# Mamba kernel on one core: the B and C rows rounded and split per half, straight from PSUM, with new orders for five queues

## The chip, the cores and the metric

The kernel runs on one core of one Trainium2 chip. The metric is the device time of one execution in microseconds (us). Before the change it is 4034.65 us, the median of three runs (4034.6 to 4036.17).

## What is computed

The reference normalises the input (4 batches of 1024 tokens, 128 features), runs two Mamba blocks over it, one forward and one over the reversed tokens, and then a transformer of six layers. The change touches the Mamba blocks alone. Cut to what matters, one of them is:

```python
xp, z = split(x @ W_in.T)                     # 256 channels each
xc = silu(causal_conv4(xp) + b_conv)
dt, Bm, Cm = split(xc @ W_x.T, [8, 24])       # 8 columns of dt, 16 of B, 16 of C
dt = softplus(dt @ W_dt.T + b_dt)
A = -exp(A_log)                               # 256 x 16
h = h * exp(dt_t * A) + (dt_t * u_t) * B_t    # per token, 256 channels x 16 states
y_t = sum over the 16 states of h * C_t
out = (y + xc * D) * silu(z) @ W_out.T
```

## The kernel before

Four batches in two directions are eight sequences of 1024 tokens, worked one behind the other; odd ones read the tokens backwards. Channels lie on partitions in two halves (h = 0, 1) of 128, tokens in the free dimension, as two PSUM banks (c = 0, 1) of 512. The recurrence runs per state: sequence s has states n = 0 to 15, and g = 16 s + n numbers them all. For each g:

- TensorE spreads the row of B for this state to all 128 partitions, into a pair of banks (`b_rows`, L345, the matmul in `row`, L341). The row lies in the tile `bc` as float32r, rounded, on partitions 0 to 31, and the rest that the rounding cut off on partitions 32 to 63; the matmul with `pick_r` adds the two.
- VectorE multiplies the pair with `dtx` for each half (`drive_half`, L488, stages dr0 and dr1). The product of half 1 goes back into the pair; that of half 0 goes to the tile `drive` in SBUF, or, for the states listed in `DRIVE_IN_PSUM`, into the other pair of banks.
- ScalarE makes the decays exp(dt * A) (`decays`, L455, stages dec0 and dec1), up to four states ahead.
- VectorE scans over the tokens (`scan`, L499, stages sc0 and sc1).
- SP fetches the row of C from HBM, spread over the partitions (`spread_c`, L284, stage cd); GpSimd multiplies the scanned state with it (`read_out`, L534, stages rd0 and rd1); TensorE adds the product to the output `y_ps` with the identity as weights (`add_read`, L362, stages y0 and y1).

Once per sequence come the projections on TensorE: x with its four taps (stages x00 to x11, half and bank), z, the B, C and dt columns (`project_bc`, L323, stages bc0 and bc1), dt (dt00 to dt11), the skip term (sk0, sk1), the output (o0, o1). ScalarE copies these out of PSUM (ax, az, abc), makes silu and softplus (abs, relu, ex, ln). GpSimd adds and multiplies for dt and dtx (ar0, tx0, ar1, tx1). VectorE gates y (gm0, gm1) and adds the output to the residual (ao0, ao1). SP stores the C rows to HBM (cst).

The B and C columns take this way: `take_bc` (L422) copies both banks from PSUM into the SBUF tile `x_dbl`; `round_bc` (L428) casts 64 partitions of 1024 columns of it into `bc`; `split_bc` (L482) subtracts, on partitions 32 to 63, the rounded values from those of `x_dbl`, with both inputs in SBUF. Then `b_rows` of the sequence may run.

Each engine's order is written out by hand as a list for one sequence (`MAMBA_PE`, `MAMBA_ACT`, `MAMBA_DVE`, `MAMBA_POOL`, `MAMBA_SP`, L104 to L147). An entry is (lag, state, stage): in round i it stands for sequence i - lag; `mamba_sequence` unrolls it. The engines work strictly in this order, and `after` puts the semaphore waits in front of each stage. A stage's two halves share one semaphore, counted in the order of the list. `mamba_slots` deals out four PSUM banks in TensorE's order: `b` alternates between the two pairs, a single projection takes a bank of the pair that the last `b` did not take, and whoever takes a bank waits for its last reader. For a projection that reader is named in `single`; for `bc0` and `bc1` it is `abc0` and `abc1`.

```python
for name, k in pe:
    other = 1 - pair
    if name == "b":
        pair = k % 2
        take("b", k, [2 * pair, 2 * pair + 1], ("sc1", k))
        if k % D_STATE in DRIVE_IN_PSUM:
            take("dr0", k, [2 - 2 * pair, 3 - 2 * pair], ("sc0", k))
    elif name in single:
        take(name, k, [2 * other + turn[other]], (single[name], k))
```

`read` and `state` have two buffers per half: rd of g waits for y of g - 2, sc of g for rd of g - 2. `mamba` is called once, at L1483; the transformer follows behind one more layer norm.

Of the kernel before, what the change touches and what calls it, by code (L numbers as in the profile page):

```python
# [43 lines left out]
def layer_norm_block(nc, ctx, sems, number, ones_mean, eps_col, src, out, work, finish, place=None, store=None):  # L44
# [70 lines left out]
MAMBA_ACT = [  # L115
# [74 lines left out]
def mamba(nc, xn, resid, c_rows, weights):  # L190
    win, wtap, wx, wdt, wout, packed, ident, pick = weights
    with ExitStack() as ctx:
# [64 lines left out]
        def banked(name, f):  # L257
            return {f"{name}{c}": f(c) for c in range(HALF_BANKS)}

        def halved(name, f):  # L260
            return {f"{name}{h}": f(h) for h in range(HALVES)}
# [1332 lines left out]
```

## Time and profile before

| | us |
|---|---|
| median of three runs | 4034.65 |
| the profiled execution | 4035.77 |
| its span, first to last instruction | 4034.0 |
| busy in the span: TensorE, VectorE, ScalarE, GpSimd | 3731, 3368, 2919, 3210 |
| Mamba: first drive of VectorE to the end of its last scan | 119.6 to 1085.3 |

The layer norms ahead of Mamba and the start of its first sequence fill the first 120 us; the transformer takes the rest, from about 1124 us on. The mean granted clock of TensorE over the span is 0.966 of full speed. In the rows below, a line of the timeline gives the start, the duration from the first start to the last end, the engine, the source line, the tiles written and read, the number of instructions merged in it, and in brackets the idle time before it and what ended it. Matmuls of 32 bits appear as two records each, so one bank of one projection with a full set of weights is two records, and `y` of one state and half is four.

### The profile page before, as it was taken

What the parts mean: (1) busy time and instruction counts of PE and PEld (TensorE: products, weight loads), DVE (VectorE), ACT (ScalarE), POOL (GpSimd) and SP (SyncE); (2) the same over time, 40 slices, a digit from 0 to 9 for tenths busy, and PEclk for the clock granted to TensorE, in tenths of its full rate; (3) what the DMA queues carried; (4) which work ended last, traced back from release to release, by engine and by line L of the source; (5) the groups of instructions that cost most, each with busy time, mean ns of one, the idle gap of its engine ahead of it and who ended that gap; (6) DMA issues with size and microseconds to landing.
All of it is one profiled execution on the core that took longest, in us unless ns stands there. A gap on an engine that the chain in (4) does not pass through costs nothing.

```text
span 4034.0 us, 110584 instructions
## 1 busy us (share of the span) xinstructions
PE 3731.3 (92%) x43424; PEld 2523.7 (63%) x43424; DVE 3367.5 (83%) x3440; ACT 2918.9 (72%) x6887; POOL 3209.6 (80%) x2362
## 2 busy tenths in 40 slices
PE   5898888888749999999999999999999999999997
PEld 2333333333337777777777777777777777677775
DVE  3799999999858887888878888888878888788885
ACT  4554555544338887888878888788888888788885
POOL 0777787777658888888888888888888888888883
PEclk8899899998879999999999999999999999999999
DMA  1121222122100000000000000000000000000001
GB/s 43 63 74 69 68 69 74 63 75 73 68 30 16 2 16 2 6 13 2 16 2 9 10 15 2 2 16 2 15 2 6 13 3 15 2 6 2 2 2 43
DMA packets 30703, 102.12 MB, mean 25 GB/s; under 512 B 4580, under 2 KB 6504, under 8 KB 29296
## 3 DMA queue, kind: packets, MB, share of 16 engines
q1 hardware_dynamic: 30192, 95.05, 6.9%
q8 instruction: 352, 5.77, 0.6%
q14 instruction: 159, 1.30, 0.1%
HBM read 90.32 MB, written 4.72 MB: 24 GB/s over the span
## 4 chain that ended last, share of the span: by engine, by line
PE 66%; issue 2%; ACT 2%; POOL 0%; DVE 0%; POOLq 0%; ACTq 0%; DVEq 0%
PE ps L979 16%; PE ps L909 13%; PE ps L968 9%; PE ps L920 8%; PE ps L956 7%; PE ps L1004 5%; PE ps L1017 3%; PE ps L941 1%; PE ps L931 1%; PE ps L986 1%; PE ps L992 1%; ACT prob L1110 0%; PE ps L891 0%; ACT mixed L1119 0%; ACT sq L1072 0%
## 5 line engine op out<-in xcount | busy, mean ns | idle before, releaser
L1365 POOL TENSOR_TENSOR resid<-resid,sq 128x1024 f32<-128x1024 f32 x384 | 909.1, 2373 | 4.2 <-DVE sq L1219 3.7
L537 POOL TENSOR_TENSOR read<-state,c_row 128x1024 f32<-128x1024 f32 x256 | 687.4, 2703 | 202.8 <-DVE state L503 132.7
L1387 POOL TENSOR_TENSOR resid<-resid,rnorm 128x1024 f32<-128x1024 f32 x384 | 725.2, 1904 | 17.8
L979 PE MATMUL ps<-mixed,w_vo 128*128 128x128 f32 x6144 | 719.1, 275 | 3.0 <-ACT mixed L1119 2.3
L979 PEld LDWEIGHTS ps<-mixed,w_vo 128*128 128x128 f32 x6144 | 709.9, 192 | 12.9 <-issue 4.6
L909 PE MATMUL ps<-w_qk,xs_parts 128*128 128x512 f32 x2304 | 639.9, 413 | 48.9 <-issue 18.9
L1110 ACT ACTIVATE prob<-ps,stat 128x64 f32<-128x64 f32 x3072 | 655.4, 384 | 0.5 <-DVE stat L1239 0.4
L1219 DVE TENSOR_TENSOR sq<-ps,rope_l 128x1024 f32<-128x1024 f32 x384 | 462.7, 1205 | 124.6 <-ACT sq L1072 124.6
L367 PE MATMUL mamba_ps<-read,ident 128*128 128x512 f32 x1024 | 521.3, 648 | 23.3 <-POOL read L537 23.0
L1232 DVE TENSOR_TENSOR resid<-ps,rope_l 128x1024 f32<-128x1024 f32 x384 | 464.8, 1210 | 71.8 <-ACT sq L1072 64.4
L909 PEld LDWEIGHTS ps<-w_qk,xs_parts 128*128 128x128 f32 x2304 | 413.6, 191 | 165.6 <-issue 82.3
L1072 ACT ACTIVATE sq<-ps 128x1024 f32<-128x1024 f32 x384 | 396.3, 1032 | 156.4 <-PE ps L909 122.1
L1394 POOL TENSOR_TENSOR prob<-prob,stat 128x1024 f32<-128x1024 f32 x192 | 365.8, 1905 | 167.6 <-DVE stat L1250 167.6
L1119 ACT COPY mixed<-ps 128x512 f32<-128x512 f32 x768 | 400.1, 603 | 112.9 <-PE ps L968 112.8
L1196 DVE TENSOR_REDUCE ssq<-sq 128x16 f32<-128x1024 f32 x384 | 465.9, 1213 | 8.9 <-ACT sq L1072 4.3
L920 PE MATMUL ps<-ident,resid 128*128 128x128 f32 x3072 | 414.8, 275 | 14.0 <-ACT w_vo L1054 13.1
L503 DVE TENSOR_TENSOR_SCAN state<-decay,mamba_ps 128x1024 f32<-128x1024 f32 x176 | 396.5, 2276 | 4.2
L920 PEld LDWEIGHTS ps<-ident,resid 128*128 128x128 f32 x3072 | 351.6, 141 | 75.5 <-issue 60.8
L968 PE MATMUL ps<-prob_t,rows 32*128 32x512 f32 x3072 | 386.2, 613 | 4.4 <-DVE xb L1267 1.6
L367 PEld LDWEIGHTS mamba_ps<-read,ident 128*128 128x128 f32 x1024 | 196.8, 203 | 294.3 <-issue 245.5
L459 ACT ACTIVATE decay<-dt,neg_a 128x1024 f32<-128x1024 f32 x256 | 279.5, 1143 | 97.6 <-DVE state L503 97.5
L1094 ACT COPY q_t<-ps 128x512 f32<-128x512 f32 x384 | 231.4, 603 | 124.7 <-PE ps L920 122.5
(140 smaller groups left out, 5724.7 us busy)
## 6 DMA issues: line engine op xcount, KB each, us to landing
c_row<-c_rows SPq DMA_DIRECT2D x128, 512.0 KB, 3.6
w_stage<-w_qk_hbm SPq DMA_DIRECT2D x6, 1024.0 KB, 4.9
vo_stage<-w_v_hbm SPq DMA_DIRECT2D x6, 512.0 KB, 3.8
vo_stage<-w_o_hbm SPq DMA_DIRECT2D x6, 512.0 KB, 4.6
xn<-x_hbm SPq DMA_DIRECT2D x4, 512.0 KB, 5.5
kept<-resid SPq DMA_DIRECT2D x8, 256.0 KB, 2.9
resid<-kept SPq DMA_DIRECT2D x8, 256.0 KB, 4.3
out_hbm<-resid SPq DMA_DIRECT2D x8, 256.0 KB, 2.0
```

What stands on the lines that cost most here:

```text
L367: last = pe.matmul(y_ps[h][:, c, :], ident[:, :], read[:, h, g % 2, cols(c)], start=False, stop=n == LAST)
L537: pool.tensor_tensor(read[:, h, g % 2, :], state[:, h, g % 2, :], c_row[:, g % C_AHEAD, :], ALU.mult).then_inc(done[f"rd{h}"], 1)
L909: last = pe.matmul(ps[:, A + c, :], xs_parts[:, odd, xpart, :], w_qk[:, wpart, cols], start=k == 0, stop=k == 2)
L920: last = pe.transpose(bank[:, j * P:(j + 1) * P], qk[:, tile % 2, col:col + P], ident[:, :])
L968: last = pe.matmul(banks[w], rows[rows_w, tile % 2, own, :], prob_t[rows_w, tile % 2, :, own, :], start=own == 0, stop=own == 1)
L979: last = pe.matmul(bank[:, 0:P], w_vo[:, l % 2, head_at(place_h), :], mixed[:, odd, place_h, :], start=place_h == 0, stop=place_h == HEADS ...
L1110: last = act.activation(prob[:, tile % 2, place_h, :], score_ps[:, place_h, :], ACT.Exp, bias=stat[:, tile % 2, 0, place_h:place_h + 1])
L1196: dve.tensor_reduce(ssq[:, tile % 2, part * HEADS:(part + 1) * HEADS, 0], sq[:, 0, :].rearrange("p (h d) -> p h d", d=HEAD_DIM), AX_X, ALU ...
L1219: dve.tensor_tensor(sq[:, 1 + part, :].rearrange("p (h s d) -> p h s d", s=2, d=HEAD_DIM // 2), swapped, table(part, 1, tile).rearrange("p ...
L1232: dve.tensor_tensor(qk[:, tile % 2, part * INNER:(part + 1) * INNER].rearrange("p (h d) -> p h d", d=HEAD_DIM), heads_ps.rearrange("p (h d ...
L1365: pool.tensor_tensor(qk[:, tile % 2, cols], qk[:, tile % 2, cols], sq[:, 1 + part, :], ALU.add).then_inc(done[f"rotated{part}"], 1)
L1387: pool.tensor_tensor(heads, heads, norms, ALU.mult).then_inc(done[f"normed{part}"], 1)
```

## The change

`round_bc` and `split_bc` now work bank by bank and read the PSUM bank of the projection: the cast (stages abch0, abch1) takes 64 partitions of 512 columns from PSUM, and the split (stages split0, split1) subtracts in two halves, with one input in PSUM and one in SBUF. `take_bc` stays, for the dt rows and the C rows. The banks of bc0 and bc1 are held until the split has read them. All five orders are new, and the list of states whose drive goes to PSUM has five members instead of six. In the diff the orders are cut: TensorE's, GpSimd's and SP's as they are after, VectorE's before and after, ScalarE's left out.

```diff
 MAMBA_PE = [
+    (2, 8, "y0"), (1, None, "dt11"), (1, None, "dt10"), (2, 11, "b"), (2, 8, "y1"), (2, 12, "b"), (2, 9, "y0"),
+    (2, 9, "y1"), (2, 10, "y1"), (2, 10, "y0"), (2, 13, "b"), (2, 11, "y0"), (2, 12, "y0"), (2, 14, "b"), (2, 11, "y1"),
+    (0, None, "x01"), (2, 13, "y0"), (2, 15, "b"), (2, 12, "y1"), (2, 13, "y1"), (2, 14, "y0"), (1, 0, "b"),
+    (2, 14, "y1"), (0, None, "x10"), (2, 15, "y0"), (1, 1, "b"), (0, None, "x11"), (2, 15, "y1"), (1, 2, "b"),
+    (0, None, "x00"), (1, None, "sk0"), (1, 3, "b"), (1, 0, "y0"), (2, None, "o1"), (1, None, "sk1"), (1, 0, "y1"),
+    (1, 4, "b"), (1, 1, "y0"), (1, 1, "y1"), (0, None, "z01"), (2, None, "o0"), (1, 2, "y1"), (1, 5, "b"), (1, 2, "y0"),
+    (0, None, "z00"), (1, 6, "b"), (1, 3, "y1"), (0, None, "bc1"), (0, None, "bc0"), (1, 3, "y0"), (1, 4, "y0"),
+    (1, 7, "b"), (1, 4, "y1"), (0, None, "z10"), (0, None, "dt00"), (1, 5, "y1"), (1, 8, "b"), (0, None, "dt01"),
+    (1, 5, "y0"), (0, None, "z11"), (1, 6, "y0"), (1, 9, "b"), (1, 6, "y1"), (1, 7, "y1"), (1, 7, "y0"), (1, 10, "b")]
...
 MAMBA_DVE = [
-    (1, 1, "dr0"), (1, 1, "dr1"), (2, None, "gm0"), (2, None, "gm1"), (1, 1, "sc1"), (1, 1, "sc0"), (1, 2, "dr0"),
-    (1, 2, "dr1"), (2, None, "ao1"), (1, 2, "sc1"), (1, 2, "sc0"), (1, 3, "dr0"), (1, 3, "dr1"), (2, None, "ao0"),
-    (1, 3, "sc1"), (1, 3, "sc0"), (1, 4, "dr0"), (1, 4, "dr1"), (1, 4, "sc0"), (1, 4, "sc1"), (1, 5, "dr0"),
-    (1, 5, "dr1"), (1, 5, "sc1"), (1, 5, "sc0"), (1, 6, "dr0"), (1, 6, "dr1"), (1, 6, "sc1"), (1, 6, "sc0"),
-    (1, 7, "dr0"), (1, 7, "dr1"), (1, 7, "sc1"), (1, 7, "sc0"), (1, 8, "dr0"), (1, 8, "dr1"), (1, 8, "sc1"),
-    (1, 8, "sc0"), (1, 9, "dr0"), (1, 9, "dr1"), (1, 9, "sc0"), (1, 9, "sc1"), (1, 10, "dr0"), (1, 10, "dr1"),
-    (1, 10, "sc0"), (1, 10, "sc1"), (1, 11, "dr0"), (1, 11, "dr1"), (1, 11, "sc0"), (1, 11, "sc1"), (1, 12, "dr0"),
-    (1, 12, "dr1"), (1, 12, "sc1"), (1, 12, "sc0"), (1, 13, "dr0"), (1, 13, "dr1"), (0, None, "split"), (1, 13, "sc1"),
-    (1, 13, "sc0"), (1, 14, "dr0"), (1, 14, "dr1"), (1, 14, "sc0"), (1, 14, "sc1"), (1, 15, "dr0"), (1, 15, "dr1"),
-    (1, 15, "sc0"), (1, 15, "sc1"), (0, 0, "dr0"), (0, 0, "dr1"), (0, 0, "sc0"), (0, 0, "sc1")]
+    (1, 3, "sc0"), (1, 4, "dr0"), (1, 3, "sc1"), (1, 4, "dr1"), (1, 4, "sc1"), (2, None, "ao0"), (1, 4, "sc0"),
+    (1, 5, "dr0"), (1, 5, "dr1"), (1, 5, "sc1"), (1, 5, "sc0"), (1, 6, "dr0"), (1, 6, "dr1"), (0, None, "split1"),
+    (1, 6, "sc0"), (0, None, "split0"), (1, 6, "sc1"), (1, 7, "dr0"), (1, 7, "dr1"), (1, 7, "sc1"), (1, 7, "sc0"),
+    (1, 8, "dr0"), (1, 8, "dr1"), (1, 8, "sc1"), (1, 8, "sc0"), (1, 9, "dr0"), (1, 9, "dr1"), (1, 9, "sc0"),
+    (1, 9, "sc1"), (1, 10, "dr0"), (1, 10, "sc0"), (1, 10, "dr1"), (1, 10, "sc1"), (1, 11, "dr0"), (1, 11, "dr1"),
+    (1, 11, "sc0"), (1, 11, "sc1"), (1, 12, "dr0"), (1, 12, "dr1"), (1, 12, "sc0"), (1, 12, "sc1"), (1, 13, "dr0"),
+    (1, 13, "dr1"), (1, 13, "sc0"), (1, 13, "sc1"), (1, 14, "dr0"), (1, 14, "dr1"), (1, 14, "sc1"), (1, 14, "sc0"),
+    (1, 15, "dr0"), (1, 15, "dr1"), (1, 15, "sc0"), (1, 15, "sc1"), (0, 0, "dr0"), (0, 0, "dr1"), (0, 0, "sc0"),
+    (0, 0, "sc1"), (0, 1, "dr0"), (0, 1, "dr1"), (1, None, "gm0"), (0, 1, "sc1"), (0, 1, "sc0"), (0, 2, "dr0"),
+    (0, 2, "dr1"), (1, None, "gm1"), (0, 2, "sc1"), (0, 2, "sc0"), (0, 3, "dr0"), (1, None, "ao1"), (0, 3, "dr1")]
...
 MAMBA_POOL = [
+    (1, 5, "rd0"), (1, 6, "rd0"), (1, 6, "rd1"), (1, 7, "rd1"), (1, 7, "rd0"), (1, 8, "rd1"), (1, 8, "rd0"),
+    (1, 9, "rd0"), (1, 10, "rd0"), (0, None, "ar0"), (1, 9, "rd1"), (1, 10, "rd1"), (0, None, "tx0"), (1, 11, "rd0"),
+    (1, 11, "rd1"), (1, 12, "rd0"), (0, None, "ar1"), (1, 12, "rd1"), (1, 13, "rd0"), (1, 13, "rd1"), (1, 14, "rd0"),
+    (1, 14, "rd1"), (0, None, "tx1"), (1, 15, "rd0"), (0, 0, "rd0"), (1, 15, "rd1"), (0, 0, "rd1"), (0, 1, "rd1"),
+    (0, 1, "rd0"), (0, 2, "rd0"), (0, 2, "rd1"), (0, 3, "rd0"), (0, 3, "rd1"), (0, 4, "rd1"), (0, 4, "rd0"),
+    (0, 5, "rd1")]
...
 MAMBA_SP = [
+    (1, 5, "cd"), (1, 6, "cd"), (1, 7, "cd"), (1, 8, "cd"), (0, None, "cst"), (1, 9, "cd"), (1, 10, "cd"), (1, 11, "cd"),
...
-DRIVE_IN_PSUM = (4, 9, 10, 11, 14, 15,)
+DRIVE_IN_PSUM = (9, 11, 12, 13, 15,)
...
-    single = {f"bc{c}": f"abc{c}" for c in range(2)} | {f"o{c}": f"ao{c}" for c in range(2)} | {
+    single = {f"bc{c}": f"split{c}" for c in range(2)} | {f"o{c}": f"ao{c}" for c in range(2)} | {
...
-                    after(pe, ("split", g // D_STATE))
+                    after(pe, ("split0", g // D_STATE), ("split1", g // D_STATE))
...
-                        after(act, (f"bc{c}", s), ("split", s - 1), ("cst", s - 1), *[(f"dt{h}{k}", s - 1) for h in range(HALVES) for k in range(2)])
+                        after(act, (f"bc{c}", s), ("cst", s - 1), *[(f"dt{h}{k}", s - 1) for h in range(HALVES) for k in range(2)])
-                def round_bc(s):
-                    after(act, ("abc0", s), ("abc1", s), ("b", D_STATE * (s - 1) - 1))
-                    act.copy(bc[:, s % 2, :], x_dbl[0:BC_ROWS, :]).then_inc(done["abch"], 1)
+                def round_bc(c):
+                    def stage(s):
+                        after(act, (f"bc{c}", s), ("b", D_STATE * (s - 1) - 1))
+                        act.copy(bc[:, s % 2, cols(c)], bank(f"bc{c}", s)[0:BC_ROWS]).then_inc(done[f"abch{c}"], 1)
+                    return stage
...
-                          **banked("abc", take_bc), "abch": round_bc, **parts("abs", take_dt("abs", ACT.Abs, dt)),
+                          **banked("abc", take_bc), **banked("abch", round_bc), **parts("abs", take_dt("abs", ACT.Abs, dt)),
...
-                def split_bc(s):
-
-                    low = bc[32:64, s % 2, :]
-                    after(dve, ("abch", s))
-                    dve.tensor_tensor(low, x_dbl[32:64, :], low.bitcast(F32), ALU.subtract).then_inc(done["split"], 1)
+                def split_bc(c):
+
+                    def stage(s):
+                        low = bc[32:64, s % 2, cols(c)]
+                        after(dve, (f"abc{c}", s), (f"abch{c}", s))
+                        dve.tensor_tensor(low, bank(f"bc{c}", s)[32:64], low.bitcast(F32), ALU.subtract).then_inc(done[f"split{c}"], 1)
+                    return stage
...
-                stages = {"split": split_bc, **halved("dr", drive_half), **halved("sc", scan),
+                stages = {**banked("split", split_bc), **halved("dr", drive_half), **halved("sc", scan),
```

## Rows read from the trace of the kernel before

**Rows 1.** VectorE's groups from first to last scan, 119.5 to 1086 us: busy, mean ns, idle

```profile
L495 DVE TENSOR_TENSOR mamba_ps<-dtx,mamba_ps 128x1024 f32<-128x1024 f32 x176 | 215.9, 1227 | 27.5 <-PE mamba_ps L342 7.8
...
L503 DVE TENSOR_TENSOR_SCAN state<-decay,drive 128x1024 f32<-128x1024 f32 x80 | 184.3, 2304 | 1.5 <-ACT decay L459 1.5
...
L495 DVE TENSOR_TENSOR drive<-dtx,mamba_ps 128x1024 f32<-128x1024 f32 x80 | 97.0, 1213 | 20.6 <-PE mamba_ps L342 14.3
...
L486 DVE TENSOR_TENSOR bc<-x_dbl,bc 32x1024 fp32r<-32x1024 f32 x7 | 19.7, 2820 | 0.2
...
L524 DVE SCALAR_TENSOR_TENSOR resid<-mamba_ps,resid 128x512 f32<-128x512 f32 x14 | 9.6, 685 | 0.0
```

**Rows 2.** Timeline of VectorE in one sequence, from 607: start us, us, what, count

```profile
607.04 1.20 DVE L495 TENSOR_TENSOR drive<-dtx,mamba_ps 128x1024 f32<-128x1024 f32 x1
...
613.95 1.19 DVE L495 TENSOR_TENSOR drive<-dtx,mamba_ps 128x1024 f32<-128x1024 f32 x1
...
623.27 1.22 DVE L495 TENSOR_TENSOR drive<-dtx,mamba_ps 128x1024 f32<-128x1024 f32 x1
...
630.96 1.22 DVE L495 TENSOR_TENSOR drive<-dtx,mamba_ps 128x1024 f32<-128x1024 f32 x1
...
653.01 1.22 DVE L495 TENSOR_TENSOR drive<-dtx,mamba_ps 128x1024 f32<-128x1024 f32 x1
...
660.29 1.22 DVE L495 TENSOR_TENSOR drive<-dtx,mamba_ps 128x1024 f32<-128x1024 f32 x1
...
682.59 2.59 DVE L495 TENSOR_TENSOR mamba_ps<-dtx,mamba_ps 128x1024 f32<-128x1024 f32 x2
...
689.68 2.59 DVE L495 TENSOR_TENSOR mamba_ps<-dtx,mamba_ps 128x1024 f32<-128x1024 f32 x2
...
696.55 1.20 DVE L495 TENSOR_TENSOR drive<-dtx,mamba_ps 128x1024 f32<-128x1024 f32 x1
...
703.80 1.22 DVE L495 TENSOR_TENSOR drive<-dtx,mamba_ps 128x1024 f32<-128x1024 f32 x1
...
706.42 2.82 DVE L486 TENSOR_TENSOR bc<-x_dbl,bc 32x1024 fp32r<-32x1024 f32 x1
709.26 2.29 DVE L503 TENSOR_TENSOR_SCAN state<-decay,mamba_ps 128x1024 f32<-128x1024 f32 x1
...
713.65 2.57 DVE L495 TENSOR_TENSOR mamba_ps<-dtx,mamba_ps 128x1024 f32<-128x1024 f32 x2
...
727.59 1.20 DVE L495 TENSOR_TENSOR drive<-dtx,mamba_ps 128x1024 f32<-128x1024 f32 x1
```

**Rows 3.** Timeline of GpSimd and VectorE around two instructions with both inputs in SBUF

```profile
671.09 2.37 POOL L537 TENSOR_TENSOR read<-state,c_row 128x1024 f32<-128x1024 f32 x1 [1.49 <-PE mamba_ps L367]
...
672.44 3.16 DVE L503 TENSOR_TENSOR_SCAN state<-decay,drive 128x1024 f32<-128x1024 f32 x1
...
701.57 6.58 POOL L537 TENSOR_TENSOR read<-state,c_row 128x1024 f32<-128x1024 f32 x2 [1.99 <-DVE state L503]
```

**Rows 4.** Timeline of VectorE: its first drive, its first scan, its last two scans

```profile
119.59 1.22 DVE L495 TENSOR_TENSOR drive<-dtx,mamba_ps 128x1024 f32<-128x1024 f32 x1 [8.81 <-PE mamba_ps L342]
...
123.63 2.29 DVE L503 TENSOR_TENSOR_SCAN state<-decay,drive 128x1024 f32<-128x1024 f32 x1 [1.45 <-ACT decay L459]
...
1080.84 4.46 DVE L503 TENSOR_TENSOR_SCAN state<-decay,mamba_ps 128x1024 f32<-128x1024 f32 x2
```

**Rows 5.** Timeline of TensorE: records behind gaps and without, in brackets the idle before

```profile
483.50 6.65 PE L311 MATMUL mamba_ps<-xn,wtap 128*128 128x512 f32 x8 [1.40 <-DVE state L503]
...
688.14 5.42 PE L367 MATMUL mamba_ps<-read,ident 128*128 128x512 f32 x12
...
1026.70 1.19 PE L342 MATMUL mamba_ps<-bc,pick_r 64*128 64x512 f32 x2 [4.65 <-DVE state L503]
1027.82 7.58 PE L367 MATMUL mamba_ps<-read,ident 128*128 128x512 f32 x12
```

**Rows 6.** Timeline of TensorE at the start: x projections ahead of the first B rows

```profile
107.85 10.18 PE L311 MATMUL mamba_ps<-xn,wtap 128*128 128x512 f32 x16
```

More of the change, by code:

```diff
@@ L104 @@
 MAMBA_PE = [
[10 rows of a table removed]
-MAMBA_ACT = [
[10 rows of a table removed]
-MAMBA_DVE = [
[10 rows of a table removed]
-MAMBA_POOL = [
[6 rows of a table removed]
[9 rows of a table added]
+MAMBA_ACT = [
[10 rows of a table added]
+MAMBA_DVE = [
[10 rows of a table added]
+MAMBA_POOL = [
[6 rows of a table added]
 MAMBA_SP = [
-    (1, 1, "cd"), (1, 2, "cd"), (1, 3, "cd"), (1, 4, "cd"), (1, 5, "cd"), (1, 6, "cd"), (1, 7, "cd"), (1, 8, "cd"),
-    (1, 9, "cd"), (1, 10, "cd"), (1, 11, "cd"), (1, 12, "cd"), (0, None, "cst"), (1, 13, "cd"), (1, 14, "cd"),
-    (1, 15, "cd"), (0, 0, "cd")]
-DRIVE_IN_PSUM = (4, 9, 10, 11, 14, 15,)
+    (1, 5, "cd"), (1, 6, "cd"), (1, 7, "cd"), (1, 8, "cd"), (0, None, "cst"), (1, 9, "cd"), (1, 10, "cd"), (1, 11, "cd"),
+    (1, 12, "cd"), (1, 13, "cd"), (1, 14, "cd"), (1, 15, "cd"), (0, 0, "cd"), (0, 1, "cd"), (0, 2, "cd"), (0, 3, "cd"),
+    (0, 4, "cd")]
+DRIVE_IN_PSUM = (9, 11, 12, 13, 15,)
 MAMBA_EXPS = ("dec0", "dec1", "ex0", "ex1", "ln0", "ln1")
```

36 rows, old and new, of tables (MAMBA_ACT, MAMBA_PE, MAMBA_POOL) are left out of this document.

## The prediction

> **What bounds the kernel now.** The change touches the Mamba part alone, so I first looked for its place in the span and for its bound. The view of instruction groups, kept to VectorE and to the stretch from the first to the last of its scans, gives few idle microseconds [rows 1]: in about 966 us the drives waited 27.5 and 20.6 us, the split 0.2. Most of that is semaphore gaps of 0.1 us; 7.8 and 14.3 us (8.8 of them ahead of the first drive) are waits for TensorE's B rows. The 80 scans of a drive in SBUF took 184.3 us, 2.7 more than 80 times 2.27. So VectorE sets the time: 256 states' worth of drive, drive, scan, scan, one behind the other. GpSimd, ScalarE and TensorE matter only where they make it wait.
>
> The timeline of VectorE shows how regular that is [rows 2]. I write dr0(g) for the first drive of state g and take the step from one dr0 to the next. From 607.04 to 727.59 is one whole sequence, 120.55 us. The steps depend only on the order within the state and on where the drive lies:
> - SBUF, scan 0 before scan 1, next drive in SBUF: 6.91 (607.04 to 613.95).
> - SBUF, scan 1 before scan 0: 7.28 (653.01 to 660.29); with two gates 9.32 (613.95 to 623.27), with one output add 7.69 (623.27 to 630.96).
> - PSUM, followed by PSUM 7.09, followed by SBUF 6.87 (682.59, 689.68, 696.55).
> - The state with the split: 9.85 (703.80 to 713.65). Its split and gap take 2.84, of which 0.05 replace a gap that would be there anyway, so without it 7.06: that is also the step of an SBUF state followed by a PSUM one.
>
> **The change, part by part.**
>
> *The split.* Before, one instruction of 1024 columns with both inputs in SBUF: 2.79 us net per sequence, 2.82 busy [rows 1, 2]. Of these 1.7 are not work: GpSimd's pair of reads that began at 701.57 ended at 708.15, and only then did the split (begun 706.42) get on, for the last 1.1 us [rows 2, 3]. The scan at 672.44 shows the same: two SBUF inputs, 3.16 us instead of 2.29, while GpSimd was in a read until 673.46 [rows 3]. Drives, with one input in PSUM, never stretch like that. After, two instructions of 512 columns with one input in PSUM; the nearest row is the output add, PSUM and SBUF in, 512 columns: 685 ns [rows 1]. How they stand between their neighbours matters. In the row, a scan starts 0.02 us after the split's end (709.24 to 709.26), whereas an independent neighbour on all partitions overlaps by 0.09 (two scans end 4.46 after 1080.84, not 4.58 [rows 4]). With these gaps on both sides one half costs 0.83, two 1.66. Were the halves to overlap like the others, two would cost 1.22; both ends go into the range. I take 1.66, for it is what this operation showed. Gain 1.13 per sequence. The first split lies ahead of the first drive, so 7 count: **-7.9 us**.
>
> The Trainium skill (VectorE: DVE Perf Modes, section Two Vector instructions with no wait between them) speaks against the halves here: an instruction whose operands start in another group of 32 partitions than the last one's is held until all before it are done, and the split starts at partition 32. The row's gap of 0.02 instead of an overlap agrees, and by the rule each half breaks the overlap twice; without the rule the sum would be 3.1 us lower (7 times 0.44).
>
> *The steps.* Without gates, outputs and splits, before: one 6.91, six of 7.28, three each of 7.06, 7.09 and 6.87, together 113.65. After: drives of five states instead of six are in PSUM (9, 11, 12, 13, 15). States 0 and 6 have scan 0 first (13.82), 1, 2, 5, 7 are 7.28 (29.12), 8 and 14 7.06 (14.12), 11 and 12 7.09 (14.18), 9, 13 and 15 6.87 (20.61), state 10, interleaved, about 7.25, states 3 and 4, interleaved so that scan 1 of state 3 stands behind dr0 of state 4, about 14.1. Sum 113.2, 0.45 less, 8 times: **-3.6 us**. Gates and outputs: before 2.04 and twice 0.41; after, the two gates stand apart (about 0.95 each) and one output lies where it covers no gap: 2.9 against 2.86, nothing.
>
> *What the timeline waits for.* Before there were 13.3 us of waiting for B rows and 2.7 us of stretched scans, 16.0 in eight sequences [rows 1]. The new orders of five queues remove them all in their old places (**-16.0**) and make new ones. I looked for these by laying the new orders of TensorE and GpSimd beside VectorE's steps.
> - State 13. `b_rows(12)` waits for scan 0 of state 11, which ends 4.75 us behind dr0(11). Between `b_rows(11)` and it TensorE has one `y` to add, 2.5 us of work at most, so it idles 2.3 us or more. Behind it stand four `y`, 16 records, and then `b_rows(13)`. At full clock: 0.63 and 16 times 0.45 (12 records took 5.42) and 0.7, so the rows are ready 13.5 us behind dr0(11); they are due at 14.16. But after such gaps the granted clock falls to the lower of its two levels, 1.2 of 2.4 GHz: behind an idle 4.65 us the B rows and 12 records took 1.12 and 7.58 where 0.63 and 5.42 is usual [rows 5], 2.65 more. That would be a wait of 2.0. I take 1.1 per sequence, between 0 and 2.0, since the gap here is nearer half as long.
> - State 15. `b_rows(14)` waits likewise, then come `y1(11)`, the four taps of `x01` (8 records), `y0(13)`: the same 16 records, due 13.93 us behind dr0(13), ready at 13.5. At the low clock 2.2 us late. The gap ahead is only 1.3 us; one x run after 1.40 us took 6.65 for its 8 records [rows 5], others did not. I take 0.6.
> - State 0. GpSimd has `tx1` ahead of `rd0(15)` and ends this read 2.83 us behind dr0(0), where the scan of an SBUF drive wants to start at 2.47. It waits, as at 672.44: 0.35.
> Together 2.05 per sequence: **+16.4 us**.
>
> *What I cost at nothing.* The two casts straight from PSUM (512 columns each, in place of one of 1024) lie on ScalarE beside the scans. The banks of `bc0` and `bc1` are now held until the splits, and `b_rows(7)` waits for the second; a scan of 2.2 us covers its 0.7 us. Without that cover it would be 0.8 us a sequence. On SP the store of the C rows moves from behind `cd(12)` to behind `cd(8)`; `cd(9)` stands behind it, but it has a state's time, and what it waits for (`abc0`) is older by then. Waits for `split` on TensorE become two on one semaphore. The two relu and abs of the last dt part move; `b_rows(11)` now waits for them, due 7.25 us behind dr0(10), with about 1 us to spare at full clock. The tail behind the last scan (at 1085.3 [rows 4]) is in the same order.
>
> *The start.* Before the first drive TensorE ran two x projections of the second sequence, 10.18 us, and the first drive stood 8.81 us waiting for B rows [rows 4, 6]. After, one of them stands there; but all four parts of dt are read ahead of it, with ScalarE's softplus between. Between -5.1 (half of 10.18) and 0, I take **-1.3**, near 0 because the longer chain of ScalarE takes most of it. The first scan then waits for its decay as before (1.45 [rows 4]).
>
> Sum: -7.9 - 3.6 - 16.0 + 16.4 - 1.3 = -12.4. The profiled execution took 4035.77 us (span 4034.0 and 1.8 around it), 1.1 above the median of the three runs. That gives 4023.4; as the runs lie a little lower, **4023**.
>
> **The rivals.**
> 1. *TensorE keeps its pace.* The new order fills the gap ahead of the x projection of state 0 with `y1(14)` (before, TensorE stood 1.40 us there and slowed [rows 5]), and the waits at 13 and 15 don't come. Then new waits are 0.35 times 8, 2.8: -26, 4010. Against it: the gaps ahead of `b_rows(11)`, `(12)` and `(14)`.
> 2. *TensorE's slow pace decides (slower).* Every long gap is followed by the low clock: 2.0 at state 13, 2.2 at state 15, about 1 at state 11, where dt, abs and relu now stand ahead of the B rows, and 0.35: 5.5 per sequence, 44 in all, +15, 4051. It is slower from new waits of 3.6 us a sequence on (28.8 in 8). For it: slack of 0.4 to 0.7 us only, against 2.65 lost per gap.
> 3. *A read gets in ahead of scan 0 of state 6.* That scan has an SBUF drive and starts 3.07 us behind dr0(6), as `rd0(5)`, released by `y0(3)`, starts at about 3.05 to 3.2. If GpSimd is first, the scan waits 2.3 us in each sequence: +18.4 on my sum, 4042.
> 4. *The split from PSUM is not freed of GpSimd.* Then each half waits for a read like the old one, 1.7 us, 14 times 1.7: +11.8, 4047. Against it: no drive ever stretched.
>
> **How the numbers follow.** Forecast 0.43, rival 1 0.25, rival 2 0.15, rival 3 0.12, rival 4 0.05. A measurement of this kernel tells about 0.2% (8 us) from no change. Faster by more: all of rival 1 and 0.32 of the forecast, 0.57. Within: 0.11 of the forecast, 0.10 of rival 3, 0.04 of rival 2: 0.25. Slower: 0.11, 0.02 and rival 4, 0.18. The range goes from 4008, rival 1 with the overlapping halves in part, to 4044, beyond rival 3; it leaves out most of rivals 2 and 4.
>
> **What would show it.** The split should have 16 instructions near 690 ns and none longer; a mean over 1 us is rival 4. The step of state 6 should be near 8.6, that of states 1 and 2 near 8.2. VectorE's waits for B rows should fall at dr0(13) and dr0(15); if they are absent and the whole sequence takes 118 us, it is rival 1. Scans of an SBUF drive over 3 us at state 6 are rival 3. A sequence above 121 us with low granted clock ahead of states 11 to 15 is rival 2. The forecast's mechanism is wrong if the split's gain is seen but the waits lie at other states.

## The result and the profile after

The changed kernel takes **4060.85 us** (median of four runs, 4058.78 to 4071.12), 1.0070 times the kernel before in the same session, 95% interval 1.0052 to 1.0088. That is 0.7% slower; 4023 was forecast, 4044 was the upper end. The profiled execution has a span of 4057.0 us against 4034.0.

Three points of VectorE's timeline split the difference of 23.0 us: the end of the last scan, the first reciprocal of the transformer's 192 tiles, and the end.

| | before | after | difference |
|---|---|---|---|
| start to end of the last scan | 1085.30 | 1071.42 | -13.9 |
| to the first reciprocal | 109.07 | 107.29 | -1.8 |
| from there to the end | 2839.6 | 2878.3 | **+38.7** |

Mamba, the only part that the change touches, got 13.9 us faster. The transformer, whose code is the same, got slower by 38.7. First Mamba. VectorE's groups from its first drive to its last scan (117.9 to 1071.5 us), answering [rows 1]:

```profile
L506 DVE TENSOR_TENSOR_SCAN state<-decay,mamba_ps 128x1024 f32<-128x1024 f32 x168 | 379.1, 2276 | 6.6 <-ACT decay L460 1.2 <-issue 0.4
L498 DVE TENSOR_TENSOR mamba_ps<-dtx,mamba_ps 128x1024 f32<-128x1024 f32 x168 | 205.7, 1225 | 28.2 <-PE mamba_ps L341 10.9 <-DVE state L506 0.5 <-DVE mamba_ps L498 0.5
L506 DVE TENSOR_TENSOR_SCAN state<-decay,drive 128x1024 f32<-128x1024 f32 x88 | 202.1, 2297 | 2.2 <-ACT decay L460 1.3
L498 DVE TENSOR_TENSOR drive<-dtx,mamba_ps 128x1024 f32<-128x1024 f32 x88 | 106.5, 1210 | 26.4 <-PE mamba_ps L341 19.6 <-DVE state L506 0.5
...
L488 DVE TENSOR_TENSOR bc<-mamba_ps,bc 32x512 fp32r<-32x512 f32 x14 | 9.6, 684 | 0.4
```

The halves of the split take 684 ns each. The 19.6 us are the wait ahead of the first drive alone; it is counted from the end of the first splits, and these now end at 98.5 us, far ahead of it (before, at 110.8). Waits for B rows inside the sequences are the 10.9 us. VectorE's timeline of one sequence around the split, and around the one state where it waits, answering [rows 2]:

```profile
641.21 1.22 DVE L498 TENSOR_TENSOR drive<-dtx,mamba_ps 128x1024 f32<-128x1024 f32 x1
642.56 1.23 DVE L498 TENSOR_TENSOR mamba_ps<-dtx,mamba_ps 128x1024 f32<-128x1024 f32 x1
643.82 0.68 DVE L488 TENSOR_TENSOR bc<-mamba_ps,bc 32x512 fp32r<-32x512 f32 x1
644.54 2.29 DVE L506 TENSOR_TENSOR_SCAN state<-decay,drive 128x1024 f32<-128x1024 f32 x1
646.86 0.68 DVE L488 TENSOR_TENSOR bc<-mamba_ps,bc 32x512 fp32r<-32x512 f32 x1
647.58 2.29 DVE L506 TENSOR_TENSOR_SCAN state<-decay,mamba_ps 128x1024 f32<-128x1024 f32 x1
649.78 1.20 DVE L498 TENSOR_TENSOR drive<-dtx,mamba_ps 128x1024 f32<-128x1024 f32 x1
...
707.76 2.59 DVE L498 TENSOR_TENSOR mamba_ps<-dtx,mamba_ps 128x1024 f32<-128x1024 f32 x2 [1.08 <-PE mamba_ps L341]
710.94 4.46 DVE L506 TENSOR_TENSOR_SCAN state<-decay,mamba_ps 128x1024 f32<-128x1024 f32 x2 [0.59 <-ACT decay L460]
```

The step of state 6 (641.21 to 649.78) is 8.57; 8.6 was forecast. The first drive starts at 118.01 and the last pair of scans at 1066.96, answering [rows 4].

Now the transformer. TensorE's idle time by line and releaser, 1120 us to the end. The line of the score matmuls (`k_t`, `q_t`) is L956 before and L959 after; "issue" is idle time for which the profile shows nothing that TensorE waited for. Before:

```profile
PE ps L956 <- issue: 4.4, 14, 0.6
```

After:

```profile
PE ps L959 <- issue: 26.9, 29, 1.6
...
PE ps L971 <- issue: 4.0, 9, 1.2
```

The timeline shows where these are. Every tile has one run of 128 records of scores. In the slow stretches one tile in four, the third of its four, has this run broken, and the number behind the `x` on the line with the gap is what was left to do behind it:

```profile
3157.18 0.34 PE L959 MATMUL ps<-k_t,q_t 64*32 64x64 f32 x15 [1.34 <-issue]
...
3215.99 0.33 PE L959 MATMUL ps<-k_t,q_t 64*32 64x64 f32 x12 [1.28 <-issue]
...
3272.16 1.40 PE L959 MATMUL ps<-k_t,q_t 64*32 64x64 f32 x119
3274.78 0.32 PE L959 MATMUL ps<-k_t,q_t 64*32 64x64 f32 x9 [1.22 <-issue]
...
3333.53 0.31 PE L959 MATMUL ps<-k_t,q_t 64*32 64x64 f32 x6 [1.25 <-issue]
...
3392.30 0.30 PE L959 MATMUL ps<-k_t,q_t 64*32 64x64 f32 x3 [1.21 <-issue]
```

15, 12, 9, 6, 3 records are left behind the gap. It stands at a place that moves by 3 records, 6 instructions, every four tiles, so it does not belong to the code at that place. Most chunks of four tiles are 1786 TensorE instructions in the compiled program and in the trace, which is 7 times 256 less 6. And the page's DMA queues have one that moves instructions:

```profile
q8 instruction: 353, 5.78, 0.6%
```

353 packets of 16.4 KB. TensorE's compiled stream is 90376 instructions of 64 bytes, 5.78 MB; so a packet is 256 instructions. Before, the stream was 90299: the changed kernel has **77 more wait instructions** on TensorE (3488 in the trace against 3411). They come from one line of the change, `after(pe, ("split0", ...), ("split1", ...))` ahead of every B row. Compiled with the second of these two waits alone, which was not run on the chip, the changed kernel has 90299 again, new orders and all. The granted clock is no cause: it reads 1.00 from 2600 to 3400 us in both kernels.

### The profile page after: what moved, and what is told of

The parts are those of the page before. It is cut to its first block, busy times and chain, and to the rows that moved or that the text cites. A ratio compares the mean times of both kernels' runs of the same rounds, so it can differ in the third digit from the quotient of the medians.

```text
span 4057.0 us, 110697 instructions
## 1 busy us (share of the span) xinstructions
PE 3731.3 (92%) x43424; PEld 2525.7 (62%) x43424; DVE 3358.6 (83%) x3448; ACT 2915.6 (72%) x6895; POOL 3193.5 (79%) x2362
## 3 DMA queue, kind: packets, MB, share of 16 engines
q8 instruction: 353, 5.78, 0.6%
## 4 chain that ended last, share of the span: by engine, by line
PE 67%; issue 2%; ACT 1%; POOL 0%; DVE 0%; POOLq 0%; DVEq 0%; ACTq 0%
PE ps L982 17%; PE ps L912 13%; PE ps L971 9%; PE ps L923 8%; PE ps L959 7%; PE ps L1007 5%; PE ps L1020 3%; PE ps L944 1%; PE ps L934 1%; PE ps L989 1%; PE ps L995 1%; PE ps L894 0%; ACT prob L1113 0%; ACT mixed L1122 0%; ACT w_vo L1057 0%
## 5 line engine op out<-in xcount | busy, mean ns | idle before, releaser
L923 PE MATMUL ps<-ident,resid 128*128 128x128 f32 x3072 | 415.2, 275 | 13.5 <-ACT w_vo L1057 13.1
L506 DVE TENSOR_TENSOR_SCAN state<-decay,mamba_ps 128x1024 f32<-128x1024 f32 x168 | 379.1, 2276 | 6.6 <-ACT decay L460 1.2
```

The source lines that it names most:

```text
L923: last = pe.transpose(bank[:, j * P:(j + 1) * P], qk[:, tile % 2, col:col + P], ident[:, :])
```

## The theory and its rival

**Stream theory**, as it stood before the experiments. TensorE's instructions come in blocks of 256. The scores of one tile are 256 instructions in 1.48 us, far denser than anything else. If a border of a block falls in or just behind them, TensorE has used up the block before the next is there, and stands 1.2 us or more. 77 instructions more ahead of the transformer moved all borders against its code, into the scores. (The last two sentences turned out too simple; the numbering behind the table shows why.) **Rival:** the transformer is slowed by something that Mamba leaves behind (the phase of the engines, another engine's stream, the clock), whatever the number of TensorE's instructions.

## Experiments on TensorE's stream

The edit of the first four runs adds waits on a semaphore that has already reached its value, at the start of the transformer's code, behind Mamba. Two such waits in the source become one instruction, so twice the number stands in the code:

```
         def _(pe):
             pe.wait_ge(const_set, CONSTS_SET)
+            for _ in range(2 * N):
+                pe.wait_ge(const_set, CONSTS_SET)
             pe.wait_ge(const_loaded, 80)
```

**The changed kernel, N = 179.**

> The changed kernel with 179 instructions more on TensorE ahead of everything, waits on a semaphore that is already there, executed while TensorE waits for the constants' DMA anyway. Stream theory: the change added 77 wait instructions to TensorE's stream; the stream comes in by blocks of 256 instructions of 64 bytes (the 16.4 KB packets of the instruction queue), and the transformer's 37 us are some 29 stalls of 1.2 to 1.5 us where the border of a block falls into the dense score matmuls of a tile. 77 + 179 is 256, so the borders fall in the transformer where they fell before: the stalls at the score matmuls go, the transformer takes about 2910 us instead of 2947, the whole about 4021 (14 below before: Mamba's own gain). Rival (the transformer is slowed by its start phase, by another engine's stream, by the order in which Mamba leaves the banks, or by the clock): nothing changes, 4057 to 4062.

Measured: 4022.93 us, ratio 0.9973 (0.9962 to 0.9984) to the kernel before, faster by 38 us than the changed kernel without the waits. Its idle time at the score matmuls:

```profile
PE ps L961 <- issue: 4.5, 13, 0.5
```

**The kernel before, N = 77.**

> The kernel before with 77 such waits on TensorE, so that its stream is as long ahead of the transformer as the changed kernel's. Stream theory: stalls of 1.2 to 1.5 us come at the same matmuls as in the changed kernel, transformer about 2947 us, whole about 4071. Rival (anything in Mamba's orders is the cause): 4035, no stall over 0.6 us at the score matmuls.

Measured: 4074.19 us, ratio 1.0094 (1.0078 to 1.0111). The stalls come at the same number of records as in the changed kernel (15, 12, 9, 6, 3, as above):

```profile
PE ps L958 <- issue: 29.4, 27, 2.0
...
3171.28 0.34 PE L958 MATMUL ps<-k_t,q_t 64*32 64x64 f32 x15 [1.31 <-issue]
...
3230.05 0.33 PE L958 MATMUL ps<-k_t,q_t 64*32 64x64 f32 x12 [1.25 <-issue]
```

The kernel before, with nothing of the change in it, now has the whole loss (2880.6 from the first reciprocal to the end). The rival falls with these two runs.

**The changed kernel, N = 256.**

> The changed kernel with 256 waits more, one block. Stream theory with a block of 256 instructions: all borders stay where they are against the code, so the time stays at 4057 to 4062 with the same stalls. Rival A (more instructions ahead of it shift the start, and any shift helps or hurts): another time, as e1. Rival B (the count of the waits itself costs): slower than 4062.

Measured: 4077.3 us in one execution, with the stalls where they were (17, 15, 12, 9, 6, 3 records). The time was expected at 4057 to 4062; most of the difference is the waits themselves, which I had taken as hidden behind the constants' DMA. TensorE's idle ahead of the transformer's first matmul was 25.41 in the changed kernel and is

```profile
PE ps L961 <- issue: 28.4, 25, 2.0
...
1139.53 3.79 PE L896 MATMUL ps<-vo_stage 64*128 64x128 f32 x32 [42.02 <-issue]
```

With 179 it was 33.72, so a wait costs (42.02 - 33.72) / 77 = 0.108 us; in the trace such waits start 0.106 apart. Of the 16.6 us of longer idle 14.1 reach the first reciprocal, which comes 121.4 us behind the last scan and not 107.3. 4077.3 - 14.1 = 4063.2 lies within the executions of the changed kernel (4058.78 to 4071.12). Rival B, that the count of waits costs something, is true for these microseconds alone. The queue of instructions moved 354 packets here, one more than in the changed kernel.

**The changed kernel, N = 90.**

> The changed kernel with 90 waits more. Stream theory: the borders drift by 6 instructions from one chunk of four tiles to the next; with 90 more they meet the score matmuls only in some 8 early chunks (tiles 8 to 24 and 52 to 56) and miss them in the later ones. So about 8 stalls instead of 29, transformer about 2920, whole about 4031, and the stalls gone behind tile 60, where the changed kernel has most of them. Rival: the same 4057 to 4062, stalls at the same tiles.

Measured: 4042.1 us in one execution, 11 above what was expected. The stalls did move to the early tiles (1182 to 1548, 1904 to 2024 us), with three more from 2440 to 2699, and are gone behind 2700, but there are 13 of 1 us or more, not 8. The window in which a border hurts is wider than I had read from the changed kernel's trace.

**Control: the kernel before, with 77 such instructions on ScalarE, VectorE and GpSimd each, none on TensorE.**

> The kernel before with 77 wait instructions more on each of ScalarE, VectorE and GpSimd at the start of the transformer, and none on TensorE. It is the control of the run with 77 on TensorE (4074). Stream theory (only TensorE's stream matters, as it alone issues 256 instructions in 1.5 us): no stall of 1.2 us at the score matmuls, 4035, plus at most some 8 us if the waits themselves delay the first tile. Rival (any stream that is shifted slows the tiles): some 4070 with stalls at the score matmuls.

Measured: 4034.23 us in one execution beside 4034.39 for the kernel before, no stall over 0.6 us at the scores:

```profile
PE ps L956 <- issue: 4.1, 12, 0.6
```

So 77 more instructions do nothing on the other three engines and cost 39 us on TensorE. Other numbers were not tried there.

**A remedy: fewer waits.** All 16 B rows of a sequence wait for its splits, though the first one's wait holds for the rest.

```
                 def b_rows(g):
-                    after(pe, ("split0", g // D_STATE), ("split1", g // D_STATE))
+                    if g % D_STATE == 0:
+                        after(pe, ("split0", g // D_STATE), ("split1", g // D_STATE))
```

> The changed kernel, where TensorE waits for the splits only ahead of the first B rows of a sequence, not ahead of all 16. That takes 120 instructions out of its stream; against blocks of 256 that is the same as 136 more. Stream theory: no stalls of 1.2 us at the score matmuls, nothing to pay for added waits, so 4018 to 4022. Rival 1 (the number of instructions alone counts, or it needs exactly the phase of the kernel before): stalls stay, 4050 to 4060. Rival 2 (the waits cost something within Mamba): the end of the last scan comes earlier than 1071.4 by over 2 us.

Measured: 4027.07 us, 0.9983 (0.9974 to 0.9992), 5 us above what was expected: two stalls at the scores are left (1266.81 and 1740.12 us). Rival 2 falls: the last scan ends at 1073.54, no earlier, so the 120 waits had cost Mamba nothing. Without them the waits for B rows even grew, to 15.9 us from 10.9, which three other runs of the changed order repeat within 0.2 (10.7 to 11.0); why was not found.

Together, all runs, those of the next section too, by TensorE instructions ahead of the transformer relative to the changed kernel; the stalls are those of 1.0 us or more in or right behind the scores:

| run | instructions | modulo 256 | stalls | first reciprocal to end, us |
|---|---|---|---|---|
| changed kernel | 0 | 0 | 18 | 2878.3 |
| before, N = 77 | 0 | 0 | 19 | 2880.6 |
| N = 256 | +256 | 0 | 19 | 2881.2 |
| split from SBUF, below | 0 | 0 | 19 | 2873.4 |
| no split, below | 0 | 0 | 19 | 2870.8 |
| N = 90 | +90 | 90 | 13 | 2860.8 |
| fewer waits | -120 | 136 | 2 | 2842.6 |
| fewer waits, other order, below | -120 | 136 | 4 | 2847.4 |
| reads moved, below | -80 | 176 | 0 | 2840.4 |
| the last order tried, below | -80 | 176 | 0 | 2840.2 |
| before | -77 | 179 | 0 | 2839.6 |
| before, 77 on the other engines | -77 | 179 | 0 | 2837.2 |
| N = 179 | +179 | 179 | 0 | 2837.1 |

The time of the untouched part follows the count modulo 256. It is not the only thing: at the same count it still differs by up to 10 us (2870.8 to 2881.2), and two kernels at 136 have 2 and 4 stalls. Of the 38.7 us, idle time at the two lines is 26.5 (26.9 and 4.0 against 4.4 and nothing listed). Of the other 12.2, 5.6 are longer busy time at the probability matmuls right behind the scores; 6.6 were not traced to a line.

**Where the stalls stand, by number.** The traces allow a stricter test than the table. Number TensorE's instructions in the order of the trace, waits, weight loads and matmuls, each matmul behind its weight load. Then the matmul behind each of the 113 stalls of the table has a number of 193, 194 or 195 modulo 256, in all eight kernels that stall, and whatever was added or taken out. So the stalls come with a border every 256 instructions. But a run of scores is itself 256 instructions, so there is such a border in each of the 192 runs of every kernel, of the kernel before too. What 77 instructions changed is which tile has it late in its run. In the changed kernel it falls behind record 96 of 128 in 23 of the runs of third tiles, and 18 of these have a gap of 0.9 us or more; in the runs of the other tiles it does so 29 times, with 2 such gaps. In the kernel before it falls there 49 times, never in a third tile, and there is no such gap. Why the third tile is the sensitive one is open: what runs ahead of its scores differs from the other tiles, but no run varied that. With N = 90 and with fewer waits some stalls are in other tiles too.

What the trace says of the mechanism: the view of DMA activity, kept to 3270 to 3278 us, has one instruction packet, at 3272.4. TensorE came to the scores at 3272.16, ran 119 records and went on at 3274.78. So a packet was moved 0.2 us into the dense run, and TensorE stood until 2.4 us behind it. The packet itself took 0.96 us and was through 0.2 us before the gap began. Over all 113 stalls TensorE goes on 2.2 to 2.9 us behind the start of the last packet. In the run with N = 179 the scores of the same tile (141 reciprocals stand ahead of it in both) begin at 3248.96, go through in 1.48 us, and the packet comes at 3250.05, when three quarters of them are done and slower work follows. The regular distance speaks for a wait on that packet; that the packet holds the very instruction that TensorE waited for, and what it waits for once the packet is through, is not shown.

The Trainium skill (Runtime: NRT & Kernel Launch, section Instruction fetch mechanics) says that an engine's code is refilled in blocks of 16 KiB, 256 instructions, while the current one runs, and that crossing a border is mostly hidden. The size agrees with the packets of 16.4 KB. That it is hidden holds for the kernel before (no stall over 0.6 us at the scores) and not for the changed one (18 stalls, each in or right behind a run of 256 instructions in 1.48 us).

## Experiments on Mamba's terms

**Does the source of the split matter?** The halves read ScalarE's copy in SBUF.

```
-                        dve.tensor_tensor(low, bank(f"bc{c}", s)[32:64], low.bitcast(F32), ALU.subtract)
+                        dve.tensor_tensor(low, x_dbl[32:64, cols(c)], low.bitcast(F32), ALU.subtract)
```

> The changed kernel, its two halves of the split reading ScalarE's copy in SBUF in place of the PSUM bank, at the same places of the order. Theory (an instruction with both inputs in SBUF is held while GpSimd is in a read; one with an input in PSUM is not): GpSimd reads from 639.2 to 643.2 and from 644.55 to 653.6 in the middle sequence of the changed kernel, so the halves get longer than 684 ns, by 1 us or more in the mean, and the last scan ends over 12 us later than 1071.4. Rival (the old split was slow for its length or its place, not for its source): 684 ns each, end of the last scan within 1 us of 1071.4.

Measured: 4068.54 us in one execution, with the stalls of the changed kernel.

```profile
L488 DVE TENSOR_TENSOR bc<-x_dbl,bc 32x512 fp32r<-32x512 f32 x14 | 23.3, 1663 | 0.4
...
652.22 4.41 POOL L540 TENSOR_TENSOR read<-state,c_row 128x1024 f32<-128x1024 f32 x1 [1.31 <-PE mamba_ps L366]
654.52 2.65 DVE L488 TENSOR_TENSOR bc<-x_dbl,bc 32x512 fp32r<-32x512 f32 x1
```

In each of the seven sequences the first half takes 0.68 us, between two reads of GpSimd, and the second 2.65, begun within a read; the step of state 6 is 10.53 against 8.57, and the last scan ends at 1085.18, 13.8 later. The second half ends 0.54 us behind the end of the read in progress (656.62), though the next read begins there at once. The stretching comes with the source, not with length or place; reading from PSUM frees the split of GpSimd.

**What does the split cost?**

> The changed kernel without the two halves of the split; the low rows of the B and C rows stay the rounded ones, so the part that corrects the rounding is left out. It prices the split: by my step the state that holds it goes from 8.57 us to 6.91 (1.66 for two halves, with the gap on both sides), by the other bound (halves overlap as other neighbours do) to 7.35. With 1.66 the last scan ends 11 to 13 us before 1071.4, less what the waits for B rows at state 13 take back.

The edit also lets the B rows wait for the casts where they waited for the splits, and frees the two banks as soon as ScalarE has read them. Measured: 4052.93 us in one execution, again with the stalls. The step of state 6 fell from 8.57 to 6.87: the two halves cost 1.70, where 1.66 was taken and 1.22 was the other bound. But the last scan ends at 1071.12, only 0.3 earlier. The saving of 11.9 us (7 times 1.70) was taken back by waits for B rows, now mostly at two states, 11 and 13:

```profile
L498 DVE TENSOR_TENSOR mamba_ps<-dtx,mamba_ps 128x1024 f32<-128x1024 f32 x168 | 205.7, 1225 | 41.5 <-PE mamba_ps L341 25.3 <-POOL dtx L554 0.5 <-DVE mamba_ps L498 0.5
```

25.3 us against 10.9. So in the changed kernel VectorE no longer sets Mamba's time alone: B rows from TensorE come too late for it to gain.

**Can these waits be ordered away?** On top of the fewer waits, two places of TensorE's order and one of ScalarE's:

```
-(2, 10, "y0"), (2, 13, "b"),
+(2, 13, "b"), (2, 10, "y0"),
...
-(2, 13, "y0"), (2, 15, "b"),
+(2, 15, "b"), (2, 13, "y0"),
...
-(0, None, "ax01"), (1, None, "sz1"), (2, 15, "dec0"),
+(2, 15, "dec0"), (0, None, "ax01"), (1, None, "sz1"),
```

> The same as the run before it, and in TensorE's order the B rows of state 13 go ahead of the first sum of state 10, those of state 15 ahead of the sum of state 13, and on ScalarE the decay of state 15 ahead of the copy of x01. Theory (behind the late B rows TensorE has 16 records where 12 would be in time): the waits for B rows at states 13 and 15, 10.9 us in the changed kernel, shrink to under 3, the two waits for a decay of 0.59 go, so 8 to 11 below the run before it, 4008 to 4013. Rival (TensorE is short of time as a whole, the wait moves to another state or to the reads): no more than 3 below it.

Measured: 4026.05 us, 0.9977 (0.9968 to 0.9986), 1.0 below the run with fewer waits alone, not 8 to 11. The waits for B rows over 0.3 us shrank to 3.7 in all, from 15.9 in the run it builds on, but in five sequences a scan of an SBUF drive now meets a run of three reads of GpSimd:

```profile
826.44 3.79 DVE L507 TENSOR_TENSOR_SCAN state<-decay,drive 128x1024 f32<-128x1024 f32 x1
...
821.10 6.98 POOL L541 TENSOR_TENSOR read<-state,c_row 128x1024 f32<-128x1024 f32 x3
```

GpSimd's reads are 2.35 us each here: the scan begins 0.71 into the third (825.73 to 828.08) and ends 2.15 behind its end. The last scan ends at 1072.48. The rival had this, no more than 3 below and the wait gone to the reads; I had not worked out its price.

**Moving the reads out of its way**, twice. First `ar1` and `tx1` behind read 0 of state 14:

> The kernel of the run with the order changed and fewer waits, in which GpSimd's two products for the next sequence (ar1, tx1) go behind its read 0 of state 14, and 40 waits more on TensorE at the start of the transformer, so that its stream is 80 instructions shorter than the changed kernel's, the same as 176 longer against blocks of 256. In the run with the order changed, scan 0 of state 14 (its drive in SBUF) took 3.79 us in place of 2.27, held by GpSimd's run of three reads. Theory: with the products moved, the reads are through before that scan, 1.5 us less in each of five to six sequences, and the product tx1 now ends about 1 us behind where the second drive of state 0 wants it, so the last scan ends at 1063 to 1070 (1072.5 there), and with no stalls at the score matmuls the whole takes 4010 to 4016. Rival (the reads are held by TensorE's sums anyway): last scan at 1072, whole 4020 to 4022.

Measured: 4045.04 us, 1.0026 (1.0016 to 1.0037), where 4010 to 4016 was expected. The last scan ends at 1094.12. The scan of state 14 is free again, but read 1 of state 14 now comes late, TensorE's sum of it stands ahead of the B rows of state 1, and the drive of state 1 waits 2.7 to 6.5 us in seven sequences. A clear miss of mine: I had followed `tx1` and not the read that it passed. Then `ar1` one place earlier:

```
-(1, 12, "rd0"), (0, None, "ar1"),
+(0, None, "ar1"), (1, 12, "rd0"),
```

> The kernel of the run with the order changed and fewer waits, with GpSimd's product ar1 one place earlier (ahead of read 0 of state 12, into 1.8 us in which GpSimd stands there), and the 40 waits at the start of the transformer of the last run. Theory: the three reads behind it then end at 23.9 to 26.3 us behind the same point where they ended at 28.1, scan 0 of state 14 is no longer held (2.27 instead of 3.79 us in five to six sequences), the step of state 14 falls from 8.6 to 7.1, the last scan ends at 1063 to 1066, and with 2840 from the first reciprocal to the end as in the last run, no stalls of 1.2 us at the score matmuls, the whole takes 4013 to 4018. Rival (the reads are bound to TensorE's sums, so that the third ends no earlier): step of state 14 stays above 8, last scan 1071 to 1073, whole about 4021.

Measured: **4020.96 us, 0.9965 (0.9951 to 0.9979)**, the best median of all runs. The scan of state 14 is 2.27 again (its step 7.06), as expected, but waits for B rows of 0.3 to 0.8 us came up at states 13, 14, 0 and 1, and scan 0 of state 0 is held in five sequences (2.69), and the last scan ends at 1073.11, not at 1063 to 1066. Its gain over the order before `ar1` was moved (4026.05) is the transformer without a stall (2840.2 against 2847.4), not Mamba. Four different kernels (the changed one, the one without a split, the one with the B rows moved forward, and this one) end their last scan within 1071.1 to 1073.1. That is hardly wider than what the changed order does by itself in four runs (1071.12 to 1073.01), so differences of 2 us there say nothing. What was freed on VectorE came back as waits for TensorE's B rows or as GpSimd's hold. TensorE's busy time from 120 to 1070 us is 820 us in the changed kernel and 838 in the one without a split, with a mean granted clock of 0.94 and 0.92. An order that relieves VectorE, TensorE and GpSimd together was not found.

## Why the prediction was wrong, by its steps

- **The step that failed** is one that I costed at nothing: "Waits for `split` on TensorE become two on one semaphore." I priced these waits by what TensorE waits in them, and they do cost Mamba nothing (taking 120 out did not bring the last scan forward). But they make 77 more instructions, all of the difference in TensorE's stream, and these moved the borders of the instruction blocks against the transformer: +38.7 us. Behind it stands the opening sentence, "the change touches the Mamba part alone", from which I took the other 2900 us as fixed. They are fixed in their code, not in their place in the stream. No rival had this.
- **The split.** 684 ns each, no half stretched, 1.70 per sequence against 1.66. Right, and the hold of the Trainium skill (VectorE: DVE Perf Modes, section Two Vector instructions with no wait between them) describes these gaps: each scan starts 0.04 behind a half's end, and the split's price is 1.70, not the 1.22 of overlapping neighbours. Rival 4 is refuted; the run from SBUF shows why.
- **The steps.** 6.84 for state 0, 8.2 for states 1 and 2, 8.57 for state 6, as listed. The sequence with no wait for B rows (the seventh) took 117.5, against 118.1 forecast without these waits (117.8 without the lock at state 0, which did not come either).
- **The new waits.** At state 13 the forecast was 1.1 times 8, 8.8 us; measured 2.65, 2.27, 1.73, 1.03 and 1.11 in five sequences, 8.8 in all. At state 15 0.6 times 8 was forecast, 4.8; two waits of 1.08 came. In sum 10.9 for 13.6: the right places, the second over-sized, and the first with too low an upper bound. It was 2.0, and its listed terms even give 13.3 and 1.8, where 13.5 and 2.0 stand; two sequences waited longer. The lock at state 0 (2.8) did not come; waits for a decay of 0.59 behind the late drive did, twice, and rival 3's held scan once, 4.00 us at state 6 of the last sequence.
- **The start.** -1.3 forecast, -1.6 measured.
- **The sum.** -12.4 was forecast; up to the last scan Mamba gave -13.9: the split -7.6 (7 times the difference of 2.79 and 1.70), the start -1.6, the old waits -16.0, the new ones +13.8 (10.9, 1.2 for the decays, 1.7 for the held scan), which leaves -2.5 for the steps, where -3.6 was forecast. With TensorE's stream put back in step (N = 179), the whole kernel measured 4022.93 where 4023 was forecast. That is not the forecast's merit: it holds only for a kernel that the change did not make, and the closeness is luck (-12.3 to the last scan, +1.6 with the added waits, -2.5 in the transformer).
- **Rivals 1 and 2** hung on TensorE's pace. Neither came in full: five sequences waited at state 13, one not at all. Rival 4's sum is 0.4 too high by its own terms (14 times 1.7 less 12.4 is +11.4), which changes nothing.

## What to carry to other kernels

When a change leaves a part untouched and that part's time moves, count each engine's instructions ahead of it. Here a stretch that issues 256 instructions in 1.48 us was sensitive to where the borders of the instruction blocks fall. The sign is a gap marked "issue" that drifts through the code at a fixed rate and stands at the same number modulo 256. The test is to add waits: to the old count modulo a block, and the time must go back; to a whole block more, and it must stay. Compare two orders of one part only with the rest at the same place modulo a block, or by that part's own end in the timeline.

Waits that an earlier wait already covers count too, even where they cost no time themselves: 77 of them cost 38.7 us here, and taking 120 out gave 34 back. Both came through the offset alone, so a kernel with such a stretch should be measured at several offsets before its time is taken for its own.

## What was not expected of the hardware

- A stall of 1.0 to 2.1 us on TensorE with nothing to wait for in the profile, up to 19 times in one execution, always at the instruction number 193 to 195 modulo 256, and ended 2.2 to 2.9 us behind the start of an instruction packet.
- A wait that is already fulfilled costs TensorE 0.108 us.
- An instruction with both inputs in SBUF that began 0.5 us or more into a read of GpSimd was held until that read ended, and not for the reads behind it: a scan of 2.27 us took 3.16, 3.79 or 4.00, each time 2.15 from the end of the read in progress (673.45, 828.08, 1002.80). The same instruction with one input in PSUM never took over 2.5 us in any run.
